# Group-norm statistics on ScalarE and GpSimd instead of VectorE, with a new plan of positions

## What is computed

```python
def _gn(v, G=32, eps=1e-5):          # 32 groups of 3 channels, over all of H and W
    g = v.reshape(B_, H_, W_, G, C_ // G)
    m = jnp.mean(g, axis=(1, 2, 4), keepdims=True)
    s = jnp.var(g, axis=(1, 2, 4), keepdims=True)
    return ((g - m) / jnp.sqrt(s + eps)).reshape(v.shape)

x = x + _L0_conv_ref(_gn(x), W1, b1, W2, b2, coef)
#   2x Fourier upsampling, h @ W1.T + b1, a quadratic per hidden unit,
#   h @ W2.T + b2, low pass, every second pixel
x = x + _L1_conv_ref(_gn(x), W_in, conv_w, conv_b, W_x, W_dt, b_dt, A_log, D, W_out)
#   tokens (4096 per sample) through a Mamba block:
#   h_t = dA_t * h_(t-1) + dBu_t ; y_t = sum_n h_t C_t ; gate with silu(z); W_out
```

## Time and profile before

| | us |
|---|---|
| median of 3 runs | 6466.51 (6453.15 to 6480.92) |
| the profiled execution | 6489.58 |
| its span, first to last instruction | 6487.5 |
| start of the first product of the scans | 340.36 |
| end of the last scan | 6470.61 |

### The profile page before, as it was taken

How to read it: one execution, slowest core, us unless ns; L and a number is a source line. 1 busy time by engine, 2 the same in 40 slices (tenths; PEclk the granted TensorE clock), 3 DMA queues, 4 the chain that set the end, 5 groups by cost and what they waited for, 6 DMA issues and landing times. The chain is left out here.

```text
span 6487.5 us, 99040 instructions
## 1 busy us (share of the span) xinstructions
PE 6116.3 (94%) x32316; PEld 3162.3 (49%) x32316; DVE 5805.0 (89%) x4698; ACT 5066.7 (78%) x8498; POOL 5193.6 (80%) x5028
## 2 busy tenths in 40 slices
PE   7999999999999999999999999999999999998776
PEld 5645545454454545545455454545545454453222
DVE  1089999999999998999999999999999999999998
ACT  4587878878787887878878788887878788786664
POOL 0078888888888887888878888888888888898888
PEclk8999999999999999999999999999999999998665
DMA  3367666666766666676666666666676666666553
GB/s 92 86 165 168 154 169 146 165 159 159 166 158 162 150 164 152 163 169 140 167 155 158 162 157 164 155 162 157 164 165 151 162 154 162 159 144 148 127 129 73
DMA packets 805825, 983.25 MB, mean 152 GB/s; under 512 B 391258, under 2 KB 417542, under 8 KB 805318
## 3 DMA queue, kind: packets, MB, share of 16 engines
q1 hardware_dynamic: 805318, 976.92, 64.1%
HBM read 717.71 MB, written 259.00 MB: 151 GB/s over the span
## 5 line engine op out<-in xcount | busy, mean ns | idle before, releaser
L1132 POOL TENSOR_TENSOR hc<-hs,cs 128x512 f32<-128x512 f32 x3072 | 3835.2, 1271 | 862.1 <-DVE hs L1103 572.6
L1103 DVE TENSOR_TENSOR_SCAN hs<-av,state,b 128x512 f32<-128x512 f32 x2688 | 3259.6, 1264 | 84.4 <-DVE b L1097 3.6
L945 ACT ACTIVATE av<-rep_d,nega 128x512 f32<-128x512 f32 x3072 | 2111.0, 713 | 35.4 <-DVE hs L1103 30.4
L1097 DVE TENSOR_TENSOR b<-rep_u,pb 128x1536 f32<-128x1536 f32 x1024 | 1801.9, 1760 | 161.3 <-PE pb L810 71.2
L819 PE MATMUL py<-hc,rsel 128*32 128x512 f32 x6144 | 1145.4, 636 | 58.1 <-POOL hc L1132 56.4
L735 PE MATMUL cb<-xu,w1a 96*128 96x392 f32 x2400 | 996.2, 517 | 23.8 <-ACT g L895 9.2
L740 PEld LDWEIGHTS cb<-w2c,g 128*98 128x98 f32 x9600 | 896.9, 169 | 164.2 <-issue 96.9
L740 PE MATMUL cb<-w2c,g 128*98 128x96 f32 x9600 | 920.6, 253 | 14.5 <-ACT g L895 11.7
L774 PE MATMUL cb<-xn,wtap 96*96 96x512 f32 x1536 | 736.9, 617 | 0.0
L895 ACT ACTIVATE g<-cb,b1a 128x392 f32<-128x392 f32 x1200 | 675.0, 580 | 66.4 <-PE cb L735 59.3
L735 PEld LDWEIGHTS cb<-xu,w1a 96*128 96x128 f32 x2400 | 416.0, 192 | 423.7 <-issue 234.1
(11 more groups left out here) (104 smaller groups left out, 6793.3 us busy)
## 6 DMA issues: line engine op xcount, KB each, us to landing
rep_d<-delta_scratch SPq DMA_DIRECT2D x512, 384.0 KB, 6.8
rep_u<-deltax_scratch SPq DMA_DIRECT2D x512, 384.0 KB, 6.6
cs<-c_scratch SPq DMA_DIRECT2D x512, 256.0 KB, 6.0
delta_scratch<-dlt SPq DMA_DIRECT2D x128, 384.0 KB, 3.1
deltax_scratch<-dlt SPq DMA_DIRECT2D x128, 384.0 KB, 7.7
t_scratch<-t1s SPq DMA_DIRECT2D x128, 300.0 KB
t1r<-t_scratch SPq DMA_DIRECT2D x160, 240.0 KB, 6.2
rr<-v_scratch SPq DMA_DIRECT2D x256, 150.0 KB
```

Of the source, the lines that this page charges most:

```text
L945: act.activation(av[:, n % NAV, :], rep_d[:, k % 2, j, :], ACT.Exp, scale=nega[:, q, j:j + 1])\
L1097: dve.tensor_tensor(b3[:, :, :], rep_u[:, k % 2, 3 * hf:3 * hf + 3, :], pb[:, None, :].broadcast_to([128, 3, T]), ALU.mult).then_inc(dve_b ...
L1103: dve.tensor_tensor_scan(hs[:, n % NHS, :], av[:, n % NAV, :], b3[:, n % 3, :], start, ALU.mult, ALU.add)\
L1132: pool.tensor_tensor(hc[:, n % NHC, :], hs[:, n % NHS, :], cs[:, k % 2, g % NQ, :], ALU.mult)\
```

## The change

The statistics leave DVE. ScalarE's copy of an `ST` bank to `xs` also gives the sum over its 512 columns (`accum_out`); a second ScalarE pass, a Square with minus the first block's mean as bias, writes into the bank and gives the sum of squares. Only then is the bank freed. For `D_lo` and `D_hi` the copies give sums, and one Square over `x1s` follows after `D_hi`. After the eighth block ScalarE makes mean and variance in four small passes. `SG1`, `SG2`, `WG` and their twins move to ScalarE, except for the power and one product (GpSimd) and `b1a`, `cst`, `wtot` (DVE). A ScalarE instruction that reads what the one before it wrote now waits for a semaphore of its own.

```diff
 AT = {
-    "act": dict(xn=8, y=(18, 6), d=13, mid=23, batch=16),
-    "pool": dict(u=23, bc=(17, 20), y=(18, 9)),
-    "sp": dict(rd=(1, 2, 3, 4), ru=(7, 9, 11, 13), cs=(15, 16, 17, 18), dl=20, du=3, x1=19, out=23),
+    "act": dict(xn=9, y=(18, 6), d=12, mid=23, batch=16),
+    "pool": dict(u=23, bc=(17, 23), y=(15, 8)),
+    "sp": dict(rd=(1, 2, 3, 4), ru=(7, 9, 11, 13), cs=(15, 16, 17, 18), dl=22, du=1, x1=21, out=23),
...
-LAG = {"pe": 0, "act": 4, "dve": 2, "pool": 1, "sp": 1}
+LAG = {"pe": 0, "act": 4, "dve": 1, "pool": 3, "sp": 1}
-W_HEAD = 72
-S_LAST, W_FIRST, W_LAST, D_FIRST, D_LAST = 86, 106, 91, 101, 136
+W_HEAD = 80
+S_LAST, W_FIRST, W_LAST, D_FIRST, D_LAST = 87, 108, 89, 98, 136
-WARM_TO = 4.8
+WARM_TO = 5.2
...
@@ ScalarE, steps @@
+                if name in ("SG1", "DG1"):
+                    act.activation(mg[:, v:v + 1], bank[0:C, 0:1], ACT.Copy, scale=-1.0).then_inc(fr, 1)
+                    act.wait_ge(fr, st.freed(i))
+                    summed(v, act.activation(dd[:, v:v + 1], mg[:, v:v + 1], ACT.Square, bias=mv[:, v, 0:1]))
+                    act.activation(vv[:, v:v + 1], dd[:, v:v + 1], ACT.Identity, bias=mv[:, v, 1:2]).then_inc(made, 1)
...
-                    act.wait_ge(xs_bn, count(xs_bn, x * 8 + b))
-                    out, src = xs[:, :], bank[0:C, :]
+                    summed(0, act.activation(xs[:, :], bank[0:C, :], ACT.Copy, accum_out=sums[:, 0, 0, b:b + 1]))
+                    squares(0, b, 512, bank[0:C, :], bank[0:C, :]).then_inc(fr, 1)
...
+            def summed(v, ins):
+                n_sum[0] += 1
+                ins.then_inc(act_sum, 1)
+                act.wait_ge(act_sum, count(act_sum, n_sum[0]))
...
+            def moments(v, n, made):
+                summed(v, act.activation(few[:, 0:n], sums[:, v, 0, 0:n], ACT.Copy, scale=1.0 / L, accum_out=mv[:, v, 0:1]))
+                summed(v, act.activation(few[:, 0:8], sums[:, v, 1, 0:8], ACT.Copy, scale=1.0 / L, accum_out=sq[:, v:v + 1]))
+                summed(v, act.activation(dd[:, v:v + 1], mv[:, v, 0:1], ACT.Square, bias=shift[:, v:v + 1]))
+                act.activation(mv[:, v, 1:2], dd[:, v:v + 1], ACT.Identity, scale=-1.0, bias=sq[:, v:v + 1]).then_inc(made, 1)
@@ VectorE, steps @@
-                    dve.bn_stats(bst[:, 0, b, :], xs[:, :]).then_inc(xs_bn, 1)
...
-                    dve.scalar_tensor_tensor(out=vv[:, v:v + 1], in0=dm[:, v:v + 1], scalar=dm[:, v:v + 1],
-                                             in1=mv[:, v, 1:2], op0=ALU.mult, op1=ALU.add).then_inc(sm, 1)
...
-                    dve.bn_stats(bst[:, 1, b, :], x1s[:, b % 2, :]).then_inc(x1_bn, 1)
```

More of the change, by code:

```diff
@@ L256, in build @@
         x1s = sb("x1s", [C, 2, T])
-        bst = sb("bst", [C, 2, 8, 6])
+        sums = sb("sums", [C, 2, 2, 16])
+        few = sb("few", [C, 16])
+        shift = sb("shift", [C, 2])
+        sq = sb("sq", [C, 2])
+        dd = sb("dd", [C, 2])
         mv = sb("mv", [C, 2, 2])
         mg = sb("mg", [C, 2])
-        dm = sb("dm", [C, 2])
         spare = sb("spare", [C, RING])
@@ L850, in step @@
             def step(st, key):
-                if key[0] in UNRINGED or key[0] in ("PAD", "SG1", "SG2", "WG", "DG", "DG1", "DG2"):
+                if key[0] in UNRINGED or key[0] in ("PAD", "DG"):
                     return
@@ L866, in step @@
                 x = st.sample(key)
+                if name in ("SG1", "DG1"):
+                    v = int(name == "DG1")
+                    made = act_dv if v else act_sv
+                    act.wait_ge(made, count(made, x * 2 + 1))
+                    act.wait_ge(pe_conv, st.done(i))
+                    act.activation(mg[:, v:v + 1], bank[0:C, 0:1], ACT.Copy, scale=-1.0).then_inc(fr, 1)
+                    act.wait_ge(fr, st.freed(i))
+                    summed(v, act.activation(dd[:, v:v + 1], mg[:, v:v + 1], ACT.Square, bias=mv[:, v, 0:1]))
+                    act.activation(vv[:, v:v + 1], dd[:, v:v + 1], ACT.Identity, bias=mv[:, v, 1:2]).then_inc(made, 1)
+                    return
+                if name in ("SG2", "DG2"):
+                    v = int(name == "DG2")
+                    act.wait_ge(pe_conv, st.done(i))
+                    act.activation(ve[:, v:v + 1], bank[0:C, 0:1], ACT.Identity, bias=eps[:, :]).then_inc(fr, 1)
+                    return
+                if name == "WG":
+                    act.wait_ge(pool_s, count(pool_s, x * 2 + 2))
+                    act.wait_ge(pe_conv, st.done(i))
+                    act.wait_ge(dve_d, count(dve_d, x))
+                    act.activation(w1a[:, :], w1t[:, :], ACT.Copy, scale=gnx[:, 0:1]).then_inc(act_w, 1)
+                    act.activation(gnd[:, :], gnx[:, :], ACT.Copy).then_inc(act_w, 1)
+                    return
                 out = None
@@ L1027, in step @@
                 name, b = key[:2]
-                if name in ("SLD", "WLD", "WARM") or name in BATCHED or name == "OUT":
+                if name in ("SLD", "WLD", "WARM", "ST", "D_hi", "SG1", "SG2", "DG1", "DG2") or name in BATCHED or name == "OUT":
                     return
@@ L1043, in step @@
                 x = st.sample(key)
[L1044 to L1074 removed]
+                if name == "WG":
+                    dve.wait_ge(pe_conv, st.done(i))
                     dve.tensor_tensor(b1a[:, :], bank[:, 0:NF], b1t[:, :], ALU.add).then_inc(fr, 1)
@@ L1119, in step @@
                         pool.wait_ge(act_gn, count(act_gn, x))
+                    else:
+                        pool.wait_ge(act_w, count(act_w, x * 2))
                     gn = gn1 if v else gnx
-                    pool.tensor_tensor(gn[:, 0:1], ve[:, v:v + 1], mhalf[:, :], ALU.pow)\
-                        .then_inc(pool_d if v else pool_s, 1)
+                    made = pool_d if v else pool_s
+                    pool.tensor_tensor(gn[:, 0:1], ve[:, v:v + 1], mhalf[:, :], ALU.pow).then_inc(made, 1)
+                    pool.wait_ge(made, count(made, x * 2 + 1))
+                    pool.tensor_tensor(gn[:, 1:2], mg[:, v:v + 1], gn[:, 0:1], ALU.mult).then_inc(made, 1)
             def unit(s, k, n):
```

90 lines of the change are left out of this document (38 added, 52 removed).

## The result

| | before | after |
|---|---|---|
| median, us | 6473.7 (6453.2 to 6486.9) | 6685.2 (6679.2 to 6689.5) |
| ratio | | 1.031, 95% interval 1.029 to 1.033 |
| span of the profiled execution | 6487.5 | 6677.4 |
| start of the scans | 340.4 | 353.6 |
| samples 1 to 13, each | 385.4 | 397.0 |

The account below looks back on a forecast made before the run. DVE sets the pace before; after, PE bounds chunks 4 to 7: 178.6 + 195.0 + 3.2 + 4.0 + 0.2 = 381.0 us a sample against 385.4. With the ends that is -64 us, scaled to 6403 us (1.0% less), range 6325 to 6485.

Parts of the forecast that it names:

- What bounds the kernel: Whole sample before: DVE sets the pace at 385.4 us, PE hardly behind; what DVE gives back below PE's need is no gain.
- Part 1, what leaves DVE: Statistics and small operations leave DVE; if DVE alone set the pace, a sample would take 359.6 us.
- Part 2, PE's need: PE asks 373.3 us a sample; DVE counts in chunks 0 to 3 (178.6), PE in 4 to 7 (195.0); 376.8 with idling.
- the running sum: Group-by-group sum of DVE's 5.58 us products and PE's priced work; adds 3.2 us of PE idling, giving 376.8 us a sample.
- Part 3, `rr`: What the running sum leaves out: the late `rr` in chunk 5 with PE's lower clock, about 4 us a sample.
- The first stays: Chunk 5: the same `rr` is still behind the store of `dlt` and two `rep_d`, so its 4.0 us a sample remain.
- The 2 us for `wtot`: Start of chunk 4: PE's wait for `wtot`, about 2 us a sample, was to go as DVE makes it one position earlier.
- Part 4, ScalarE: ScalarE takes over squares, sums and small passes, 13 to 25 us a sample; busy 328 to 340 of 381, it stays below PE.
- I price the leak at 0.2 us: Banks of `ST` or `D_hi` freed a square later may hold PE: 0.2 us for the whole sample, at most 8.
- The ends: Outside the 14 regular samples: start 8 us longer, sample 14 10 us less, sample 15 unchanged.
- ScalarE becomes the bound: Slower rival: squares make banks and `av` late, from 0.28 us per square; 390.4 us a sample, 6534 us, chance 0.17.
- The gain is eaten: No-change rival: PE bounds half the sample, one more `rr` can be late; 385 us a sample, 6460 us, chance 0.22.

Follow-up runs that it names:

- e10_before_rr3: The kernel before with three buffers for `rr` instead of two: 6420.3 us, 0.990 of before.
- e6_code_no_squares: The new statistics on the old positions, each square made over one column, so the norms are wrong: 6490.3 us, 1.001 of before.
- e9_after_rr3: The changed kernel with three buffers for `rr` instead of two, nothing else moved: 6473.5 us, 0.998 of before.
- e4_fewer_warm: The changed kernel with `WARM_TO` 4.8 as before, so fewer filler matmuls: 6667.6 us, 1.027 of before.
- e16_before_rr3_dld: The kernel before with three `rr` buffers and the step for `wtot` and the first `rr` loads three positions earlier: 6436.1 us, 0.993 of before.
- e14_new_late_rr3_pad: e11_at_back_rr3_pad with ScalarE's chain for mean and variance after the copy of `SB` 7 instead of after `ST` 7: 6370.5 us, 0.983 of before.
- e11_at_back_rr3_pad: The changed kernel with `AT` and `LAG` of before (GpSimd's lag 3), three `rr` buffers and `PAD` moved to chunk 0: 6413.8 us, 0.989 of before.

## Why the prediction was wrong, by its own steps

**What bounds the kernel**: right. With `rr` in time DVE waits only 10.6 us for `pb` in the whole run of `e10_before_rr3`. And below PE's need nothing is a gain: `e6_code_no_squares`, with DVE's work gone and no squares, is as fast as before.

**Part 1, what leaves DVE**: 273 us of busy time, 17 a sample in the mean of 16; the text had 20.

**Part 2, PE's need**: right where PE is the bound. With `rr` in time (`e9_after_rr3`) chunks 4 to 7 take 197.6 us, and the running sum has 198.1. Chunks 0 to 3, for which the text took DVE's number, take 185.1 against 178.4; that belongs to part 4. The whole sample of `e9_after_rr3`, 382.7 us, is near the forecast's 381.0 by luck: 4.0 us for `rr` in the one stand against 5.7 us of other things in the other. The fillers' price, 5.4 us a sample, counted against the bound, but without them a sample is only 0.2 us shorter and the kernel 0.4% faster (`e4_fewer_warm`): they lie where PE has time.

**Part 3, `rr`**: this is the step that failed. "The first stays" priced wait and clock at 4 us a sample, from the `rr` in chunk 5. For the kernel before that price holds: the third buffer takes 4.4 us off its sample. But the text compared the positions of that late load alone and did not do the same for the first ones, though `D_FIRST` 98 moves all sixteen: by SP's order the third `rr` now stands behind three `rep_d`. In after the third buffer takes 14.3 us off a sample, so the term was short by 10.3 us of the 16.0 between forecast (381.0) and result (397.0). It would have been enough to turn the sign: 4.4 us less become 5.9 more. The other 5.7 us are still there in `e9_after_rr3`.

The 2 us for `wtot` are not shown to be a gain. The wait is gone in after, but taken away from before (`e16_before_rr3_dld`) it gives nothing; another small operation comes late in its place.

**Part 4, ScalarE**: the durations were nearly right. A square of 512 columns takes 0.654 us (PSUM) or 0.687 (`x1s`), a small pass 0.155 to 0.295 (the text's least was 0.193), and ScalarE is busy 334.1 us in the stretch of 394 from 1908 us. The upper bound for a sum output, 0.19, is what it is. The rows, groups of after:

```profile
L960 ACT ACTIVATE cb<-x1s,shift 96x512 f32<-96x512 f32 x128 | 88.0, 687 | 4.2
L960 ACT ACTIVATE cb<-cb,shift 96x512 f32<-96x512 f32 x128 | 83.7, 654 | 4.2
...
L934 ACT ACTIVATION_READ_ACCUMULATOR x1s<-cb,cst 96x1 f32 x256 | 49.0, 191 | 0.0
```

The estimate from the Trainium skill (ScalarE: Activation LUTs, What ACT_TABLE_LOAD costs) was 0.71, near the measured value and a little high. What was wrong is "I price the leak at 0.2 us". 70 us of idle time in a sample did not cover what ScalarE does ahead of a copy that frees a bank: on the old positions the squares cost 0.30 to 0.39 us each, above the 0.28 from which the text let that rival decide. On the new ones they cost 0.7 us a sample, and the chain after `ST` 7 costs 3.2, measured by moving it (`e14_new_late_rr3_pad`, on the old `AT`). These two are 3.9 of the 5.7 us a sample that `rr` leaves; the rest stays open. All is inside "at most 8", and the value taken was the lower end. This is the second step that failed, and the smaller one.

**`PAD`**: as said, in chunk 7 with PE as the bound; 53.7 us, "over 50". `e11_at_back_rr3_pad` shows that little of it is a loss: with `PAD` moved, 4.0 us leave chunk 7 and 3.2 come back in chunk 0.

**The ends**: the start grew by 13.2 us, not 8; without the squares by 9.2. Sample 14 was to fall by 10 and rose by 4.9; with `rr` in time it falls by 5.6. Sample 15 was to stay and rose by 4.6, through `AT`, which the text did not cost.

**Rivals**: "ScalarE becomes the bound" named the right side, but not the size: its squares give 0.7 us a sample in the changed kernel. "The gain is eaten" had the mechanism, "one more `rr` can be late", but for another load and too cheap: it meant the one behind all four `rep_d`, which waits 12.3 us in the run, not the third, which waits 72.0, and with the forecast's 4.0 it had 8.0 us a sample for `rr` where the buffer gives back 14.3.

**What would show it**: VectorE's wait for `pb` (670 us, mostly chunks 4 to 7), chunk 7, `wtot` and ScalarE's busy time came as said. Chunks 0 to 3 "longer than 46 us (ScalarE)" is what chunk 3 did (49.0), and `e14_new_late_rr3_pad` puts 3.5 us of it down to ScalarE's chain.

## What to carry to other kernels

When a plan moves steps, list for each moved step the load that it needs and what stands ahead of that load in its queue, for the first step of a stage as for the last. A load that is late where the matmul engine is the bound costs its wait and more: here 133 us of waits and 87 us of matmuls at the lower clock, together 3.3% of the kernel, and a third buffer removed nearly all of it. That an engine idles a fifth of the time does not make it free to put work ahead of a copy that frees a bank: squares of 0.65 to 0.69 us on ScalarE cost 0.30 to 0.39 us each on the old positions. And when a forecast and a repaired kernel agree, add up the terms: two errors can hide each other.
